# A six-layer graph network on one core: one TensorE semaphore per step in passes 1 to 4, and dense blocks streamed in 13 parts through four buffers

## Chip, core and metric

The kernel runs on one core of a Trainium2 chip, in one launch. The metric is device time in microseconds. Three timed runs of the kernel before gave 6187.99, 6189.50 and 6197.62 us, median 6189.5 us.

## What is computed

A graph of 6250 nodes with 256 features and 106250 edges (source, target, weight), sorted by target, goes through six layers with a sparse product each. Cut to what matters here:

```
A(h) = segment_sum(h[src], dst);  Aw(h) = segment_sum(w * h[src], dst);  LN = layer norm of rows
x = LN(x + rows_to_length_one(x @ Ws.T + Aw(x) @ Wn.T))                     # pass 0
h = x
for i in 0..2: h = relu(LN(relu(((1 + eps[i]) * h + A(h)) @ W1[i] + b1[i]) @ W2[i] + b2[i] + h) * gamma[i] + beta[i])   # 1 to 3
x = LN(x + h)                                                               # end of pass 3
y = (A(x * deg_out**-.5) * deg_in**-.5) @ Wgc + bgc + x @ Wres + bres       # pass 4
x = LN(x + batchnorm(y + top-2 mixture of 64 experts(y)))                   # expert stage
out = LN(x + (x - Aw(x) * (diag + 1)) @ W + bias)                           # pass 5
```

What matters for the change is A in passes 1 to 4: the same unweighted adjacency matrix times a new table of rows in each pass.

## The kernel before, in words

The targets are 49 tiles (NT) of 128 nodes. In passes 1 to 4, 29 of them are "sparse" tiles and 20 (ND) are "dense" tiles.

**Sparse tiles.** A tile has 18 columns of 128 edges, handled in six groups (GT) of three columns. For each group POOL gathers the source rows by indirect DMA (`gather`, L2228), DVE builds three one-hot "pick" matrices (`picks`, L2892, two groups ahead), and TensorE multiplies them (`products`, L2299 in passes 1 to 4, L2302 elsewhere): rows are kept as three bf16 planes, so a group is nine matmuls of 128x128 by 128x256. Slots and picks have three groups of buffers; gather and picks of group n wait on `s_prod` for the products of group n-3. A pass has 174 groups.

**Dense tiles.** For a dense tile the whole block row of the adjacency matrix, 49 blocks of 128x128 in bf16, was written to DRAM in pass 0 (`dense_blocks`, `a_dram`). In every pass from 1 to 4, TensorE multiplies all 20 x 49 = 980 blocks by the planes in SBUF (`dense`, L2323): three matmuls a block. The blocks are streamed by SP's DMA queue in QN = 10 parts per tile of four or five blocks (`load_quarter`, L2060) into three buffers AB, one in `ring` and two in `pick`. TensorE raises `s_dq` at a part's last matmul; SP waits for part n-3 before it loads part n; TensorE waits on `s_al` at a part's first block.

**The order of the work** is written out by hand as steps. `one_pass` (L2461) of TensorE in passes 1 to 4 has 183 steps: first the dense blocks of the step, six or seven of them in the first 162 (DSTEPS), then the nine products of group g, in pass 2 also six histogram matmuls (L2402), then the events of the step, then block ranks (L2331, L2335). Events belong to finished tiles: T transposes of the sums (L2417), H hidden layer (L2426), L second layer (L2441), and in pass 4 GT (L2450) and G (L2458) for the gate. They follow a tile's last product at fixed offsets (`OFFSETS`): a sparse tile ends at a step that is 5 modulo 6 and a dense tile's place is rounded up to 2 modulo 6, so that a step has at most one of T, H and L in passes 1 to 3, and at most one of them with one of GT and G in pass 4. Each kind raises a semaphore of its own: `s_prod`, `s_dq`, `s_hist`, `s_t`, `s_mm1`, `s_mm`, `s_gate`, `s_lg`.

The other engines walk through the same steps. DVE in step g builds the picks of group g+2, then does the row work of its events: Z (operand, from the finished sums), F (layer norm), R and M (splitting rows into planes), then background work (sorting edges into bins, one-hots). ScalarE copies transposes (L2627) and hidden layers (L2634) out of PSUM and takes roots (L2656). SP's queue issues in order, in each step: the parts whose buffer `quarter_done_at` places in that step, then own rows (L2052), finished rows (L2036, L2032), new planes (L2045), and rows of planes for the next pass (L2075). It reads:

```
def quarter_done_at(a):
    i, q = divmod(a, QN)
    return ((i * NT + QB[q + 1]) * DSTEPS - 1) // (ND * NT)

def blocks(g):
    return range(-(-g * ND * NT // DSTEPS), -(-(g + 1) * ND * NT // DSTEPS)) if g < DSTEPS else range(0)
```

Of the kernel before, what the change touches and what calls it, by code (L numbers as in the profile page):

```python
# [1383 lines left out]
QN = 10  # L1384
# [49 lines left out]
def gnn(nc, a, out):  # L1434
# [4 lines left out]
    with ctx:  # L1439
# [107 lines left out]
        s_al = [sem(f"dense_quarter{j}_loaded") for j in range(3)]  # L1547
        s_dq = sem("dense_quarters_done")
# [8 lines left out]
        s_prod = sem("product_groups_done")  # L1557
# [3 lines left out]
        s_mm1 = sem("first_products_done")  # L1561
# [10 lines left out]
        s_hist = sem("source_histograms_done")  # L1572
# [4 lines left out]
        s_gate = sem("gate_inputs_transposed")  # L1577
        s_gatec = sem("gate_transposes_copied")
        s_lg = sem("logits_done")
# [50 lines left out]
        AB = [v.bitcast(bf16) for v in (ring[:, SLOTS * HST // 2:SLOTS * HST // 2 + AW], pick[:, AT_AB:AT_AB + AW], pick[:, AT_AB + AW:AT_AB + 2 * AW])]  # L1630
# [229 lines left out]

        def total(k, p, w=D):

            _, q, kind, i = SEQ[k][p]
            if kind == "dense":
                n = (k - 1) * ND + i
                return bank(5 + n % 2, w), s_dq, QN * (n + 1)
# [3 lines left out]
            return bank((sparse_before(k) + i) % 2, w), s_prod, group(k, i * GT + GT - 1) + 1  # L1870
# [89 lines left out]
        def _(sp):  # L1960
# [93 lines left out]
            def load_quarter(k, a):  # L2054
                i, q = divmod(a, QN)
                n = (k - 1) * ND * QN + a
                if n >= 3:
                    sp.wait_ge(s_dq, n - 2)
                w = (QB[q + 1] - QB[q]) * P
                sp.dma_start(AB[n % 3][:, 0:w], a_dram[i][:, QB[q] * P:QB[q + 1] * P]).then_inc(s_al[n % 3], 16)  # L2060

            def load_rows(k, r):
# [7 lines left out]
                if r == 0 and k > 1:  # L2070
                    sp.wait_ge(s_dq, QN * ND * (k - 1))
# [6 lines left out]
            for k in range(5):  # L2078
# [6 lines left out]
                for q in range(3 if k in DENSE_PASSES else 0):  # L2085
# [4 lines left out]
                if k == 3:  # L2090
                    sp.wait_ge(s_hist, NH)
# [33 lines left out]
            sp.wait_ge(s_dq, QN * ND * 4)  # L2125
# [70 lines left out]
        def _(pool):  # L2196
# [71 lines left out]
        def _(pe):  # L2268
# [17 lines left out]
            def products(k, g):  # L2286
# [16 lines left out]
                last.then_inc(s_prod, 1)  # L2303

            def dense(k, g):
                for b in blocks(g):
# [6 lines left out]
                    if t == QB[q]:  # L2313
                        pe.wait_ge(s_al[quarter % 3], 16 * (quarter // 3 + 1))
# [5 lines left out]
                    block = AB[quarter % 3][:, (t - QB[q]) * P:(t - QB[q] + 1) * P]  # L2320
# [4 lines left out]
                    if t == QB[q + 1] - 1:  # L2325
                        last.then_inc(s_dq, 1)
# [72 lines left out]
            def histogram(g):  # L2399
# [4 lines left out]
                last.then_inc(s_hist, 1)  # L2404

            def transposes(k, p):
# [11 lines left out]
                last.then_inc(s_t, 1)  # L2418

            def hidden(k, q):  # L2420
# [7 lines left out]
                last.then_inc(s_mm1, 1)  # L2428

            def layer(k, q):  # L2430
# [11 lines left out]
                last.then_inc(s_mm, 1)  # L2442

            def gate_transposes(p):
# [6 lines left out]
                last.then_inc(s_gate, 1)  # L2451

            def gate(p):
# [5 lines left out]
                last.then_inc(s_lg, 1)  # L2459

            def one_pass(k):  # L2461
                for g in range(STEPS[k]):
                    if k in DENSE_PASSES:
                        dense(k, g)
                    if g < GROUPS[k]:
                        products(k, g)
# [4 lines left out]
                    if k == 2 and 5 <= g < 5 + NH:  # L2471
                        histogram(g - 5)
# [119 lines left out]
        def _(act):  # L2592
# [18 lines left out]
            def operand(p):  # L2611
# [3 lines left out]
                if n:  # L2615
                    act.wait_ge(s_t, n)
                fn(TZ[:, :], sums, ACT.Copy).then_inc(s_z, 1)

            def copy_transposes(k, q):
                n = nth(k, q)  # L2620
                act.wait_ge(s_t, n + 1)
                if k in (1, 2, 3) and q:
                    act.wait_ge(s_mm1, hid(k, q))
                elif n:
                    act.wait_ge(s_mm, n)
# [3 lines left out]
            def hidden(k, q):  # L2629
                act.wait_ge(s_mm1, hid(k, q) + 1)  # L2630
                if hid(k, q):
                    act.wait_ge(s_mm, nth(k, q))
# [817 lines left out]
```

## Time and profile before

| | |
|---|---|
| Timed runs, median of 3 | 6189.5 us (6187.99 to 6197.62) |
| Profiled execution, span | 6792.0 us |
| Mean granted TensorE clock | 0.902 |
| Setup and pass 0 | 0 to 1268 us |
| Pass 1 | 1268 to 2095 us |
| Pass 2 | 2095 to 2925 us |
| Pass 3 | 2925 to 3790 us |
| Pass 4 | 3790 to 4590 us |
| Routing, experts, batch norm, pass 5 | 4590 to 6792 us |
| TensorE matmuls in the span | 36004, busy 5260.0 us (77%) |

The profiled execution is one run under the hardware profiler; its span, from the first to the last instruction, is 602 us more than the median of the timed runs, and the profile gives no other time for it. Times of single instructions and waits come from that execution. PE is TensorE, PEld its weight loads. A wait is written as engine, its line, "<-" and what ended it: total us, times, longest. "issue" means that nothing in the profile ended the wait, "remote" a semaphore event without a releaser found.

### The profile page before, as it was taken

The numbers are of one execution on the slowest core, as the hardware profiler recorded it, in microseconds if no ns is written. First come the engines' busy times: TensorE is split into PE (matmuls) and PEld (weight loads), VectorE is DVE, ScalarE is ACT, GpSimd is POOL, SyncE is SP. The second block draws the span as 40 slices with busy tenths as digits, with TensorE's granted clock in tenths as the row PEclk, the third lists the DMA queues.
The fourth block names the chain that finished last, engine by engine and source line by source line (L and its number), as shares of the span: only waits on it lengthen the run. The fifth ranks groups of instructions, "written<-read, shape, count | busy, mean of one in ns | idle before, by whom it ended". The sixth has DMA issues, their size and how long they took to land. (4 is left out here: it accounts for less than half of the span.)

```text
span 6792.0 us, 104767 instructions
## 1 busy us (share of the span) xinstructions
PE 5260.0 (77%) x36004; PEld 4236.7 (62%) x36004; DVE 3784.2 (56%) x13501; ACT 1674.7 (25%) x4718; POOL 3742.9 (55%) x3737
## 2 busy tenths in 40 slices
PE   5888876688887888868887688880399965878787
PEld 3666664576765777647776577760388853666665
DVE  5666665476675878647776211124277745444443
ACT  3766764011110111112121000000133322222222
POOL 6666666566665666656666566651300042666665
PEclk8989997799998999989999899995699977899998
DMA  5333444666667777776666666651599952333333
GB/s 141 121 119 122 129 125 130 200 197 196 197 199 239 227 226 227 235 230 185 188 187 202 201 185 182 185 162 60 196 316 310 318 171 77 97 97 96 96 98 85
DMA packets 702175, 1180.94 MB, mean 174 GB/s; under 512 B 131306, under 2 KB 510312, under 8 KB 698924
## 3 DMA queue, kind: packets, MB, share of 16 engines
q0 software_dynamic: 212192, 625.22, 32.2%
q1 hardware_dynamic: 489450, 548.94, 25.2%
q8 instruction: 295, 4.83, 0.3%
q14 instruction: 238, 1.95, 0.1%
HBM read 1010.58 MB, written 164.46 MB: 173 GB/s over the span
## 5 line engine op out<-in xcount | busy, mean ns | idle before, releaser
L2228 POOL DMA_INDIRECT ring<-planes,REC x2088 | 2080.7, 997 | 1259.5 <-issue 542.1
L2323 PE MATMUL PS<-HH,pick 128*128 128x256 bf16 (+1 forms) x7836 | 1047.4, 278 | 193.8 <-issue 154.4
L2228 POOL DMA_INDIRECT ring<-in_x,REC x738 | 797.0, 1080 | 416.3 <-issue 195.4
L2892 DVE TENSOR_SCALAR pick<-ring,REC 128x128 bf16<-128x128 bf16 x2088 | 422.5, 265 | 1074.3 <-remote 792.7
L2323 PEld LDWEIGHTS PS<-HH,pick 128*128 128x128 bf16 x7836 | 765.5, 100 | 384.8 <-issue 221.9
L2302 PE MATMUL PS<-ring,pick 128*128 128x256 f32 x2880 | 857.5, 429 | 187.3 <-DMA ring<-table,REC 96.9
L2299 PE MATMUL PS<-ring,pick 128*128 128x256 bf16 (+1 forms) x6264 | 854.3, 279 | 104.1 <-issue 55.9
L2228 POOL DMA_INDIRECT ring<-table,REC x702 | 671.7, 957 | 454.2 <-issue 301.9
L2302 PEld LDWEIGHTS PS<-ring,pick 128*128 128x128 f32 x2880 | 573.6, 212 | 379.5 <-DMA ring<-table,REC 127.4
L2299 PEld LDWEIGHTS PS<-ring,pick 128*128 128x128 bf16 x6264 | 611.3, 99 | 249.3 <-issue 113.0
L2890 DVE TENSOR_SCALAR pick<-iota,REC 128x128 f32<-128x128 f32 x1440 | 414.7, 354 | 574.9 <-remote 272.1
L2323 PE MATMUL PS<-HH,ring 128*128 128x256 bf16 (+1 forms) x3924 | 543.8, 279 | 120.5 <-issue 84.8
L2323 PEld LDWEIGHTS PS<-HH,ring 128*128 128x128 bf16 x3924 | 383.7, 100 | 213.3 <-issue 116.7
L2251 POOL DMA_INDIRECT ring<-expert_outputs,ring x98 | 96.5, 985 | 706.0 <-DMA expert_outputs<-ring 664.7
L2385 PE MATMUL PS<-HH 128*128 128x256 f32 x1764 | 453.1, 402 | 22.1 <-ACT HH L2685 17.8
L2345 PE MATMUL PS<-HH 128*128 128x256 f32 (+3 forms) x1400 | 343.7, 362 | 125.7 <-ACT HH L2718 63.2
L2385 PEld LDWEIGHTS PS<-HH 128*128 128x128 f32 x1764 | 355.1, 204 | 80.7 <-ACT HH L2685 13.6
L2627 ACT ACTIVATE TZT<-PS 128x256 f32<-128x256 f32 (+1 forms) x294 | 132.5, 451 | 973.7 <-remote 552.9
L2345 PEld LDWEIGHTS PS<-HH 128*128 128x128 f32 (+1 forms) x1400 | 214.1, 165 | 204.5 <-issue 94.9
L2441 PE MATMUL PS<-WA,TZT 128*128 128x256 f32 x980 | 276.7, 422 | 61.5 <-ACT TZT L2627 46.7
L2529 PE MATMUL PS<-ring,HH 128*128 128x128 f32 x2240 | 277.5, 278 | 0.3 <-issue 0.3
L2441 PEld LDWEIGHTS PS<-WA,TZT 128*128 128x128 f32 x980 | 202.6, 214 | 108.6 <-ACT TZT L2627 55.6
(352 smaller groups left out, 7721.0 us busy)
## 6 DMA issues: line engine op xcount, KB each, us to landing
HH<-in_L_gnn_w SPq DMA_DIRECT2D x280, 512.0 KB, 5.1
pick<-dense_blocks SPq DMA_DIRECT2D x480, 160.0 KB
ring<-dense_blocks SPq DMA_DIRECT2D x240, 160.0 KB
HH<-planes SPq DMA_DIRECT2D x64, 576.0 KB
ring<-planes,REC POOLq DMA_INDIRECT x2088
dense_blocks<-HH SPq DMA_DIRECT2D x20, 1568.0 KB
planes<-pick SPq DMA_DIRECT2D x147, 192.0 KB
expert_inputs<-VEC SPq DMA_DIRECT2D x41, 512.0 KB
```

Source lines behind the costliest of these rows:

```text
L2228: pool.indirect_dma_start(SLOTB[:, slot, 0:RP] if dense else SLOT[:, slot, 0:D], None, planes[k] if dense else tables[k], bass.IndirectOff ...
L2251: pool.indirect_dma_start(ring[:, n % 8 * D:(n % 8 + 1) * D], None, ys_dram, bass.IndirectOffsetOnAxis(ap=GI[:, s * NT + t:s * NT + t + 1] ...
L2299: last = mm(bank(j % 2, w), PICKB[:, slot * P:(slot + 1) * P], SLOTB[:, slot, PLANE_AT[m]:PLANE_AT[m] + w], start=c == 0 and m == 0, stop= ...
L2302: last = mm(bank(j % 2, D), pick[:, slot * P:(slot + 1) * P], SLOT[:, slot, 0:D], start=c == 0, stop=c == WT - 1)
L2323: last = mm(bank(5 + n % 2, w), block, plane(m, t, w), start=t == 0 and m == 0, stop=t == NT - 1 and m == 2, skip_group_check=True)
L2345: last = mm(bank(b, w, j * 2 * P), sources[slot][:, j * P:(j + 1) * P], targets[slot][:, j * 2 * P:j * 2 * P + w], start=True, stop=not ow ...
L2385: last = mm(bank(sums_bank(v), D), AW32[f % OWN][:, s % 4 * P:(s % 4 + 1) * P], tile(X, s), start=pos == 0 and s == sources[0], stop=pos = ...
L2441: last = mm(bank(layer_bank(k), D), v, wmat(m, b), start=i == 0, stop=i == len(pairs) - 1)
L2529: last = mm(bank(3 + j, P, m * P), W1B[j][:, b * HID + m * P:b * HID + (m + 1) * P], XTB[j][:, b * P:(b + 1) * P], start=b == 0, stop=b == 1)
L2627: fn(TZT[:, 0:w], bank(2, w), ACT.Copy).then_inc(s_zt, 1)
L2890: last = v.tensor_scalar(p, iota[:, :], lo, we, ALU.is_equal, ALU.mult)
L2892: last = v.tensor_scalar(p, iotab, lo, None, ALU.is_equal)
```

## The change

In passes 1 to 4 TensorE raises only `s_prod`, once in each step that has products or an event, at the last matmul of that work. `WORK[k]` lists these steps (177, 177, 177 and 178 in passes 1 to 4). `s_dq`, `s_hist`, `s_mm1`, `s_gate` and `s_lg` are gone; `s_t` and `s_mm` stay for passes 0 and 5. Whoever waited for one of them, or for a group's products, waits for the count of its step. The dense blocks of a tile are cut into QN = 13 parts of three or four blocks, held in QA = 4 buffers; SP loads a part when the step that `quarter_done_at` gives for the part four before it is done. Block ranks still come after the increment. The diff, cut (waits of the histogram, gate, hidden layer and layer change in the same manner as those shown):

```diff
-QN = 10
+QN = 13
+QA = 4
...
+STEP_OF = [{(n, p): g for g, found in EVENTS[k].items() for n, p in found} for k in range(PASSES)]
+WORK = [sorted(set(range(GROUPS[k])) | {g for g, found in EVENTS[k].items() for n, _ in found
+                                        if k in DENSE_PASSES and n in ("T", "H", "L", "GT", "G")}) for k in range(PASSES)]
...
-        s_al = [sem(f"dense_quarter{j}_loaded") for j in range(3)]
-        s_dq = sem("dense_quarters_done")
+        s_al = [sem(f"dense_part{j}_loaded") for j in range(QA)]
...
-        s_prod = sem("product_groups_done")
+        s_prod = sem("tensor_steps_done")
...
-        AB = [v.bitcast(bf16) for v in (ring[:, SLOTS * HST // 2:SLOTS * HST // 2 + AW], pick[:, AT_AB:AT_AB + AW], pick[:, AT_AB + AW:AT_AB + 2 * AW])]
+        AB = [v.bitcast(bf16) for v in [ring[:, SLOTS * HST // 2:SLOTS * HST // 2 + AW]] +
+              [pick[:, AT_AB + j * AW:AT_AB + (j + 1) * AW] for j in range(QA - 1)]]
...
+        def step_done(k, g):
+
+            return sum(len(WORK[j]) for j in range(k)) + sum(w <= g for w in WORK[k])
+
+        def pass_done(k):
+            return step_done(k, WORK[k][-1])
+
+        def group_done(n):
+
+            k = next(k for k in range(PASSES) if n < GBASE[k + 1])
+            return step_done(k, n - GBASE[k])
+
+        def event_done(name, k, p):
+
+            return step_done(k, STEP_OF[k][name, p])
+
+        def transposed(n):
+            k, p = divmod(n - 1, NT)
+            if k in DENSE_PASSES:
+                return s_prod, event_done("T", k, p)
+            return s_t, p + 1 + (NT if k == 5 else 0)
+
+        def layer_done(n):
+            k, p = divmod(n - 1, NT)
+            if k in DENSE_PASSES:
+                return s_prod, event_done("L", k, p)
+            return s_mm, p + 1 + (NT if k == 5 else 0)
+
+        def hidden_done(n):
+            k, p = divmod(n - 1, NT)
+            return s_prod, event_done("H", k + 1, p)
+
         def total(k, p, w=D):
 
             _, q, kind, i = SEQ[k][p]
...
             if kind == "dense":
                 n = (k - 1) * ND + i
-                return bank(5 + n % 2, w), s_dq, QN * (n + 1)
+                return bank(5 + n % 2, w), s_prod, step_done(k, quarter_done_at(QN * i + QN - 1))
             if kind == "weighted":
                 v = SUMMED.index((k, q))
                 return bank(sums_bank(v), w), s_wq, NB * (v + 1)
-            return bank((sparse_before(k) + i) % 2, w), s_prod, group(k, i * GT + GT - 1) + 1
+            return bank((sparse_before(k) + i) % 2, w), s_prod, step_done(k, i * GT + GT - 1)
...
             def load_quarter(k, a):
                 i, q = divmod(a, QN)
                 n = (k - 1) * ND * QN + a
-                if n >= 3:
-                    sp.wait_ge(s_dq, n - 2)
+                if a >= QA:
+                    sp.wait_ge(s_prod, step_done(k, quarter_done_at(a - QA)))
+                elif k > 1:
+                    sp.wait_ge(s_prod, step_done(k - 1, DSTEPS - 1))
                 w = (QB[q + 1] - QB[q]) * P
-                sp.dma_start(AB[n % 3][:, 0:w], a_dram[i][:, QB[q] * P:QB[q + 1] * P]).then_inc(s_al[n % 3], 16)
+                sp.dma_start(AB[n % QA][:, 0:w], a_dram[i][:, QB[q] * P:QB[q + 1] * P]).then_inc(s_al[n % QA], 16)
...
                 if r == 0 and k > 1:
-                    sp.wait_ge(s_dq, QN * ND * (k - 1))
+                    sp.wait_ge(s_prod, step_done(k - 1, DSTEPS - 1))
...
                     if k in DENSE_PASSES:
-                        for q in range(3, ND * QN):
-                            if quarter_done_at(q - 3) == g:
+                        for q in range(QA, ND * QN):
+                            if quarter_done_at(q - QA) == g:
                                 load_quarter(k, q)
...
                 if n >= 3:
-                    pool.wait_ge(s_prod, n - 2)
+                    pool.wait_ge(s_prod, group_done(n - 3))
...
-                last.then_inc(s_prod, 1)
+                if k not in DENSE_PASSES:
+                    last.then_inc(s_prod, 1)
+                return last
...
                     if t == QB[q]:
-                        pe.wait_ge(s_al[quarter % 3], 16 * (quarter // 3 + 1))
+                        pe.wait_ge(s_al[quarter % QA], 16 * (quarter // QA + 1))
...
-                    if t == QB[q + 1] - 1:
-                        last.then_inc(s_dq, 1)
...
-                last.then_inc(s_hist, 1)
+                return last
...
-                last.then_inc(s_t, 1)
+                if k not in DENSE_PASSES:
+                    last.then_inc(s_t, 1)
+                return last
...
             def one_pass(k):
                 for g in range(STEPS[k]):
                     if k in DENSE_PASSES:
                         dense(k, g)
+                    last = None
                     if g < GROUPS[k]:
-                        products(k, g)
+                        last = products(k, g)
                     if g == 1:
                         pe.wait_ge(s_w, w_count(k))
                         if k == 0:
                             pe.wait_ge(s_wtc, 1)
                     if k == 2 and 5 <= g < 5 + NH:
-                        histogram(g - 5)
+                        last = histogram(g - 5)
                     if k == 4 and g == 3:
                         pe.wait_ge(s_bad, 1)
                         mm(bank(7, 1)[0:1, :], ones[:, 0:1], col[:, 11:12], start=True, stop=True)
@@ -2477,15 +2516,17 @@
                         mm(bank(7, NT, 128)[0:1, :], ones[:, 0:1], HELD5, start=True, stop=True).then_inc(s_badp, 1)
                     for name, p in events(k, g):
                         if name == "T":
-                            transposes(k, p)
+                            last = transposes(k, p)
                         if name == "H":
-                            hidden(k, p)
+                            last = hidden(k, p)
                         if name == "L":
-                            layer(k, p)
+                            last = layer(k, p)
                         if name == "GT":
-                            gate_transposes(p)
+                            last = gate_transposes(p)
                         if name == "G":
-                            gate(p)
+                            last = gate(p)
+                    if k in DENSE_PASSES and g in WORK[k]:
+                        last.then_inc(s_prod, 1)
...
                 if n:
-                    act.wait_ge(s_t, n)
+                    act.wait_ge(*transposed(n))
...
                 if n >= 3:
-                    dve.wait_ge(s_prod, n - 2)
+                    dve.wait_ge(s_prod, group_done(n - 3))
```

## Rows read from the trace of the kernel before

**Rows 1.** The page: its first line, busy time by engine, clock and DMA slices.
```profile
span 6792.0 us, 104767 instructions
...
PE 5260.0 (77%) x36004; PEld 4236.7 (62%) x36004; DVE 3784.2 (56%) x13501; ACT 1674.7 (25%) x4718; POOL 3742.9 (55%) x3737
...
PEclk8989997799998999989999899995699977899998
DMA  5333444666667777776666666651599952333333
```

**Rows 2.** Busy time by stretch: setup and pass 0, then passes 1 to 4.
```profile
core 0: us, PE busy (x) PEld busy (x) DVE busy (x) ACT busy (x) POOL busy (x), PEclk, DMA share, GB/s
0.00:1268.00 1268.00, 926.25 (x4280) 726.47 (x4280) 785.55 (x2646) 732.51 (x1982) 808.32 (x760) 0.88 0.43 133
1268.00:2095.00 827.00, 693.60 (x5492) 564.41 (x5492) 558.41 (x1989) 103.13 (x354) 537.08 (x515) 0.92 0.68 200
2095.00:2925.00 830.00, 692.58 (x6074) 554.96 (x6074) 584.38 (x2877) 91.71 (x296) 503.13 (x524) 0.95 0.76 230
2925.00:3790.00 865.00, 679.73 (x5472) 564.69 (x5472) 593.00 (x2128) 162.05 (x497) 542.61 (x525) 0.92 0.66 196
3790.00:4590.00 800.00, 687.73 (x5394) 563.92 (x5394) 163.04 (x676) 49.10 (x99) 489.41 (x518) 0.97 0.63 182
```

**Rows 3.** Waits of PE in 1300 to 4530 us: total, times, longest.
```profile
PE PS L2323 <- issue: 238.6, 367, 20.7
...
PE PS L2299 <- issue: 53.4, 109, 1.6
PE PS L2299 <- DMA ring<-planes,REC: 39.7, 28, 3.6
PE PS L2323 <- DMA pick<-dense_blocks: 36.2, 17, 15.9
PE PS L2441 <- ACT TM L2634: 28.5, 16, 5.2
...
PE PS L2426 <- ACT TZT L2627: 12.5, 12, 2.8
...
PE PS L2323 <- DMA ring<-dense_blocks: 8.5, 8, 3.4
```

**Rows 4.** Timeline of PE in pass 3: a whole step and its neighbours.
```profile
start us, us, engine line op out<-in xcount [idle before <-releaser]
3016.86 1.16 PE L2426 MATMUL PS<-TZT,WA 128*128 128x128 f32 x8 [0.21 <-issue]
3017.85 2.14 PE L2323 MATMUL PS<-HH,pick 128*128 128x256 bf16 x18
3019.83 1.15 PE L2299 MATMUL PS<-ring,pick 128*128 128x256 bf16 x9
3020.82 1.03 PE L2441 MATMUL PS<-WA,TM 128*128 128x256 f32 x4
...
3025.14 2.14 PE L2323 MATMUL PS<-HH,pick 128*128 128x256 bf16 x18
3027.11 1.15 PE L2299 MATMUL PS<-ring,pick 128*128 128x256 bf16 x9
3028.10 1.15 PE L2323 MATMUL PS<-HH,pick 128*128 128x256 bf16 x9
```

**Rows 5.** Timeline, pass 4: a load of a dense part and its wait.
```profile
4193.38 0.32 SPq L2060 DMA_DIRECT2D ring<-dense_blocks  x1
...
4193.96 0.38 PE L2450 MATMUL PS<-ident,HN 128*128 128x128 f32 x2
...
4195.95 0.28 PE L2323 MATMUL PS<-HH,ring 128*128 128x256 bf16 x1 [0.29 <-DMA ring<-dense_blocks]
```

**Rows 6.** Timeline, pass 1: loads behind a queue, and the wait for one.
```profile
1346.28 1.89 SPq L2060 DMA_DIRECT2D pick<-dense_blocks  x2
...
1349.54 0.82 PE L2323 MATMUL PS<-HH,pick 128*128 128x257 bf16 x3 [1.22 <-DMA pick<-dense_blocks]
```

**Rows 7.** Waits of SP's DMA queue in 1300 to 4530 us.
```profile
SPq L2060 <- remote: 1128.8, 272, 13.7
SPq L2060 <- PE PS L2323: 978.4, 342, 12.7
SPq L2036 <- DVE HN L3201: 80.2, 27, 8.7
SPq L2045 <- DVE pick L3076: 53.4, 18, 12.1
...
SPq L2032 <- DVE HN L3173: 10.0, 2, 9.5
```

**Rows 8.** Waits of DVE in 1300 to 4530 us.
```profile
DVE pick L2892 <- remote: 772.7, 273, 6.9
DVE pick L2892 <- PE PS L2299: 230.2, 104, 20.4
```

More of the change, by code:

```diff
@@ L2084, in _ @@
                     sp.dma_start(SRCI[0:EP, 0:EC], a["src"].rearrange("(p c) -> p c", c=EC)).then_inc(s_in, 16)
-                for q in range(3 if k in DENSE_PASSES else 0):
+                for q in range(QA if k in DENSE_PASSES else 0):
                     if k == 1 and q == 0:
@@ L2319, in dense @@
                         pe.wait_ge(s_rl[r % 3], 16 * (r // 3 + 1))
-                    block = AB[quarter % 3][:, (t - QB[q]) * P:(t - QB[q] + 1) * P]
+                    block = AB[quarter % QA][:, (t - QB[q]) * P:(t - QB[q] + 1) * P]
                     for m in range(3):
@@ L2427, in hidden @@
                                   start=d == 0, stop=d == 1)
-                last.then_inc(s_mm1, 1)
+                return last
             def layer(k, q):
@@ L2441, in layer @@
                     last = mm(bank(layer_bank(k), D), v, wmat(m, b), start=i == 0, stop=i == len(pairs) - 1)
-                last.then_inc(s_mm, 1)
+                if k not in DENSE_PASSES:
+                    last.then_inc(s_mm, 1)
+                return last
             def gate_transposes(p):
@@ L2450, in gate_transposes @@
                     last = nc.tensor.transpose(bank(3, P, b * P), HN[:, o + b * P:o + (b + 1) * P], ident[:, :])
-                last.then_inc(s_gate, 1)
+                return last
             def gate(p):
@@ L2458, in gate @@
                     last = mm(bank(7, NE), TM1[:, b * P:(b + 1) * P], WG[:, b * NE:(b + 1) * NE], start=b == 0, stop=b == 1)
-                last.then_inc(s_lg, 1)
+                return last
             def one_pass(k):
@@ L2620, in copy_transposes @@
                 n = nth(k, q)
-                act.wait_ge(s_t, n + 1)
+                act.wait_ge(*transposed(n + 1))
                 if k in (1, 2, 3) and q:
-                    act.wait_ge(s_mm1, hid(k, q))
+                    act.wait_ge(*hidden_done(hid(k, q)))
                 elif n:
-                    act.wait_ge(s_mm, n)
+                    act.wait_ge(*layer_done(n))
                 w = 2 * D if k in (0, 4) else D
@@ L2629, in hidden @@
             def hidden(k, q):
-                act.wait_ge(s_mm1, hid(k, q) + 1)
+                act.wait_ge(*hidden_done(hid(k, q) + 1))
                 if hid(k, q):
-                    act.wait_ge(s_mm, nth(k, q))
+                    act.wait_ge(*layer_done(nth(k, q)))
                 for b in range(2):
@@ L2640, in finish @@
                 if k == 0:
-                    act.wait_ge(s_mm, n + 1)
+                    act.wait_ge(*layer_done(n + 1))
                     if n:
@@ L2664, in gate_copy @@
             def gate_copy(p):
-                act.wait_ge(s_gate, p + 1)
+                act.wait_ge(s_prod, event_done("GT", 4, p))
                 if p:
-                    act.wait_ge(s_lg, p)
+                    act.wait_ge(s_prod, event_done("G", 4, p - 1))
                 fn(TM1[:, :], bank(3, D), ACT.Copy).then_inc(s_gatec, 1)
@@ L3146, in operand @@
                 dve.wait_ge(s, value)
-                dve.wait_ge(s_t, n)
+                dve.wait_ge(*transposed(n))
                 if k in (1, 2, 3):
@@ L3166, in finish @@
                 hn = HN[:, m % 2 * D:(m % 2 + 1) * D]
-                dve.wait_ge(s_mm, n + 1)
+                dve.wait_ge(*layer_done(n + 1))
                 if k == 4:
@@ L3213, in one_pass @@
                 if k == 1:
-                    dve.wait_ge(s_prod, group(1, 0))
+                    dve.wait_ge(s_prod, pass_done(0))
                     for j in range(2):
@@ L3336, in _ @@
             last.then_inc(s_route, 1)
-            dve.wait_ge(s_prod, group(5, 0))
+            dve.wait_ge(s_prod, pass_done(4))
             dve.wait_ge(s_b1t, 1)
```

16 lines of the change are left out of this document (6 added, 10 removed).

## Prediction

> **What bounds the kernel now.** I read the page first [rows 1]: TensorE is busy 77% of a span of 6792.0 us, more than any other engine, but unevenly. The busy time by stretch [rows 2] shows where the change acts: passes 1 to 4 take 827, 830, 865 and 800 us, 3322 in all, and TensorE has 680 to 694 us of work in each, against 537 for POOL at most and 593 for DVE. Passes 1 to 4 are bound by TensorE's own stream; a gain or a loss there is a gap taken out of that stream or put into it. The waits of TensorE [rows 3] say what the gaps are today: the largest name no releaser (238.6 us before the dense products of L2323, 53.4 before the edge products of L2299), gathers 39.7 us, hidden layers 28.5 and 12.5, and the loads of dense parts only 36.2 + 8.5 = 44.7 us in 25 gaps, 15.9 of it a single one. So three buffers of five blocks nearly hide the stream of dense blocks. The timeline of a step [rows 4] gives the pace: 18 dense matmuls (six blocks) in 1.98 us from start to start, 0.33 us a block; nine edge products in 0.99 us; then one event, 0.99 us for a hidden layer (L2426), about 1.0 for a layer (L2441), 0.38 for a pair of transposes as in [rows 5]; 0.8 on average. What stands behind the dense blocks in a step, its tail, is 0.99 + 0.8 = 1.8 us.
>
> **Semaphore increments.** TensorE raises in passes 1 to 4 696 increments after groups of products, 800 after dense parts, 637 after events (4 x 49 T, 3 x 49 H, 4 x 49 L, 49 GT, 49 G) and 147 after histograms: 2280. Of them 3 x 177 + 178 = 709 stay, so 1571 go. Their price by the rows: the run of 18 at 3025.14 covers six blocks, a part has at most five, so it has a part's increment inside, and its 18 starts take 1.97 us, as the others do; nine products that end in one take 0.99 us to the next dense matmul, 0.110 us each, the same pace [rows 4]. I take 0 us. The rows are rounded to 0.01 us, so either sign of 0.01 x 1571 = 16 us is the bound.
>
> The Trainium skill speaks here for a gain: TensorE: Matmul & The Clock Gate, section "The cost: per-tile semaphore tail", says that increments on completing matmuls serialize, at 26.3 ns each. By that figure, as an estimate, 1571 fewer would give 41 us back. The rows above do not show it.
>
> **Later signals to those who follow products.** The gathers (POOL, L2228) and picks (DVE, L2892) of group n wait for group n-3. They now wait until the event of that step is over, 0.8 us later on average. Both work with three groups of buffers, two steps ahead, a step being 827/183 = 4.5 us in the trace. DVE waits 1003 us before its picks [rows 8], and TensorE's list holds no wait for a pick at all; that cover hides it: 0 us. If it were gone, each of the 28 gaps for a gather would grow by 0.8 us, 22 us, and the 28 gaps for ScalarE's copies (16 + 12) by as much, since DVE stands in the same order before its row work: another 22. T, H, L and GT or G signals lie at the end of their step anyway, alone in it in passes 1 to 3; block ranks come after the increment. The histogram's followers already wait for that step's products. 0 us; upper bound 44, and nothing below 0, because no signal comes earlier than now.
>
> **The stream of dense parts.** This is the term that counts. A freed buffer is refilled by SP, and the question is how much TensorE work lies between the release and the first matmul of the refilled part.
> - Before: the part is released by its own last matmul, and two parts, 9 or 10 blocks, lie between. In a pass 197 loads are made so; 154 have two tails between and 43 have one: 3.2 + 3.6 = 6.8 or 3.2 + 1.8 = 5.0 us, mean 6.5.
> - After: the release is the end of the step that `quarter_done_at` names. Three parts lie between, but the rest of the step is spent before the release. That function rounds up: where a part's last block is the last of its step, it names the next step for 39 of 256 loads. Counted through the schedule, 32 loads of a pass have no tail left and 5 blocks (28) or 6 (4): 1.65 or 1.98 us, mean 1.7. The other 224 have one tail and 6 to 11 blocks: 3.8 to 5.4 us, mean 4.6.
> - What a load needs: one is issued by SP at 4193.38 and TensorE gets on at 4195.95, 2.57 us [rows 5]; another goes from 1346.28 to 1349.54, 3.26 us [rows 6]. Both are of 160 KB against some 120 KB after; I take 2.9, their mean.
> - The 32 short ones: 4 x 32 = 128 times 2.9 - 1.7 = 1.2 us is 154 us. The ends: 0, if smaller parts land in 1.7 us, and 128 x (3.26 - 1.65) = 206.
> - The 896 others: cover falls from 6.5 to 4.6 us. Today's 25 gaps arise where SP was late too; SP stands behind DVE's rows 27 + 18 + 2 = 47 times, up to 12.1 us [rows 7], while for 2107 us it stands ready at a load's wait. Leaving out the single gap of 15.9 us, 24 gaps grow by 1.9 us each: 46 us. The ends: 0, and all 47 stands, 89 us.
> - SP issues 240 loads more in the four passes, at 0.32 us each [rows 5]: 77 us in a queue that waits 2107, hidden; that cover gone they are inside the 89 above. Waiting for a step's end before the stores of that step holds these back by up to a tail; rows are read again only in the next pass, own rows only some steps later: 0, bound by the same 89.
>
> The Trainium skill weighs in on the load: DMA: Bandwidth & Descriptors, section "Anatomy of one DMA — SWDGE (gpsimd) path", puts a transfer at a fixed 2.0 us plus its bytes over 436 GB/s. As an estimate 128 KB would take 2.3 us, the short loads would cost 128 x 0.6 = 77 us, and the sum below would be 77 us less. The trace's own two loads are longer, by their rows.
>
> **Absorbed.** While TensorE waits for a part, gathers and copies catch up. The gaps that can shrink are 39.7 + 28.5 + 12.5 = 81 us; I take half, 40, with 0 and 81 as ends.
>
> **Sum:** 0 + 0 + 154 + 46 - 40 = +160 us. The profiled execution has a span of 6792.0 us and would have 6952; it is 602 us above the median of the timed runs, 6189.5, so the nameless gaps are likely to be smaller there. I carry the 160 over unchanged: 6189.5 + 160 = 6350 us, 2.6% slower. Between the ends: -16 - 81 gives -97; 16 + 44 + 206 + 89 gives +355.
>
> **Rivals.**
> - *The increments cost what the nameless gaps show (faster).* TensorE has 238.6 + 53.4 = 292 us of gaps with no releaser before its products [rows 3]. If they belonged to the increments, 1571/2280 of them, 201 us, would go, and the loads would give back only part: -201 + 160 = -41, 6148 us. It decides from the point where an increment costs over 160/1571 = 102 ns. For it: the gaps are there, and nothing else is named. Against it: the runs with an increment inside keep their pace [rows 4], and the timed runs are 602 us shorter than the profiled one, so that much of these gaps may belong to the profile. With the page's 26.3 ns it would be 160 - 41 = +119, 6308 us, still slower.
> - *The loads stay hidden (no change).* If SP's part lands within the 1.7 us, or the four buffers spare the 24 gaps of now and the rest is absorbed: 6190, within 12 us. Against it: neither load in the rows lands under 2.57 us.
> - *The step becomes a lock (much slower).* SP, POOL and DVE all hang on the step's end; if all ends of above come together, +300 to +355 us, about 6510. For it: DVE has 593 us of work in pass 3, its chain is long. Against: rows 8.
> - *The change does less than it says:* 709 of 2280 increments stay by the schedule, so that is excluded; but the loads' release may fall a step late in more cases than counted, which is the case above.
>
> **Chances.** Forecast 0.55 (6230 to 6450), lock 0.13, hidden 0.12, increments 0.20. A difference under 0.2%, 12 us, can't be told from none. Faster 0.20, same 0.12, slower 0.68. The range leaves out the greater part of the lock and half of the faster rival: 6150 to 6460.
>
> **What would show it.** Right: TensorE's waits for dense_blocks rise from 25 gaps to 100 or more, of 1 to 2 us, to some 200 us in all, spread over the four passes in a pattern of the schedule; TensorE's work per pass stays at 680 to 694 us, and its passes grow by 30 to 50 us each; pass 0, the experts and pass 5 stay. Wrong: if the nameless gaps shrink by two thirds the increments were the cost; if waits for gathers and copies grow instead of those for dense blocks, the late signals were; if loads land in under 1.7 us, nothing happens.

## The result, and the profile after

The changed kernel takes 6323.55 us (median of 4 runs, 6318.07 to 6328.31) against 6192.35 us for the kernel before on the same chip: a ratio of 1.0219, 95% interval 1.0203 to 1.0235. It is slower by 131 us. The two medians alone give 1.0212, inside the interval, so what is worked out below from 1.0219 may be 4 us too large. Forecast were 6350 us and +160 us over 6189.5.

The first profiled execution of the kernel before was unusual: no other profile here has a span so far from its timed runs as 6792.0 us. So the kernel before was profiled once more (first experiment), and this second profile, of 6189.1 us, is what the profile of after is set against. The page of after, its first lines:

```profile
span 6321.1 us, 105019 instructions
...
PE 5082.1 (80%) x36004; PEld 4181.5 (66%) x36004; DVE 3773.7 (60%) x13501; ACT 1679.3 (27%) x4718; POOL 3737.9 (59%) x3737
...
PEclk8999998899998999989999899995699997899998
DMA  5433434677778878876666776661599972333333
```

And of the kernel before in its second profile:

```profile
span 6189.1 us, 104767 instructions
...
PE 5061.4 (82%) x36004; PEld 4192.1 (68%) x36004; DVE 3774.7 (61%) x13501; ACT 1677.1 (27%) x4718; POOL 3743.3 (60%) x3737
...
PEclk8999998799998999989999899975799987899998
DMA  5443434677778888876666777751799962444433
```

The work is the same, 36004 matmuls; TensorE is busy 21 us longer, the span is 132 us longer. Busy time by stretch, after: setup and pass 0, passes 1 to 4, the rest (columns as in [rows 2]):

```profile
0.00:1213.50 1213.50, 917.81 (x4280) 713.44 (x4280) 785.79 (x2646) 733.06 (x1982) 807.51 (x760) 0.89 0.45 139
1213.50:1955.20 741.70, 644.33 (x5493) 548.17 (x5494) 555.21 (x1989) 105.97 (x354) 545.95 (x521) 0.96 0.76 226
1955.20:2726.10 770.90, 659.58 (x6075) 559.20 (x6076) 566.45 (x2877) 94.83 (x296) 496.98 (x523) 0.95 0.80 247
2726.10:3544.10 818.00, 662.39 (x5472) 560.81 (x5473) 592.55 (x2128) 162.90 (x497) 538.31 (x521) 0.93 0.69 206
3544.10:4255.00 710.90, 651.63 (x5374) 559.70 (x5375) 153.00 (x667) 42.76 (x96) 487.66 (x515) 0.98 0.69 200
4255.00:6321.00 2066.00, 1546.36 (x9314) 1240.22 (x9313) 1120.73 (x3194) 539.78 (x1493) 861.54 (x898) 0.88 0.53 166
```

The same for the kernel before, second profile, passes 1 to 4 and the rest:

```profile
1211.90:1957.80 745.90, 646.86 (x5492) 548.89 (x5493) 557.18 (x1989) 103.69 (x354) 553.91 (x522) 0.95 0.75 226
1957.80:2663.20 705.40, 645.72 (x6074) 557.93 (x6074) 565.20 (x2877) 92.31 (x296) 499.19 (x521) 0.96 0.86 269
2663.20:3466.00 802.80, 664.02 (x5472) 565.51 (x5472) 591.87 (x2128) 162.35 (x497) 533.02 (x522) 0.92 0.70 210
3466.00:4122.20 656.20, 641.29 (x5373) 560.27 (x5374) 153.96 (x667) 47.05 (x96) 487.83 (x515) 0.99 0.74 216
4122.20:6189.00 2066.80, 1542.87 (x9315) 1239.76 (x9314) 1119.89 (x3194) 538.90 (x1493) 860.84 (x898) 0.88 0.54 166
```

The loss lies in passes 2 (+65.5 us) and 4 (+54.7); pass 3 loses 15.2, pass 1 gains 4.2, and what is outside them stays within 2 us. Waits of TensorE over the whole span, after (columns as in [rows 3]):

```profile
PE PS L2359 <- DMA pick<-dense_blocks: 149.7, 114, 4.4
...
PE PS L2359 <- DMA ring<-dense_blocks: 96.2, 45, 26.5
...
PE PS L2333 <- DMA ring<-planes,REC: 71.6, 67, 3.8
...
PE PS L2359 <- issue: 55.4, 3, 19.8
PE PS L2462 <- ACT TZT L2668: 50.9, 30, 4.6
```

And before, second profile:

```profile
PE PS L2299 <- DMA ring<-planes,REC: 98.9, 118, 5.0
...
PE PS L2426 <- ACT TZT L2627: 63.2, 36, 6.0
PE PS L2323 <- issue: 55.6, 3, 19.7
PE PS L2323 <- DMA pick<-dense_blocks: 51.2, 27, 17.7
PE PS L2323 <- DMA ring<-dense_blocks: 38.9, 11, 26.7
```

TensorE waits for dense parts 159 times instead of 38, and 245.9 us instead of 90.1: +155.8 us. It waits 27.3 us less for gathers (L2333, L2299 before) and 12.3 us less for transposes copied by ScalarE. 155.8 less 27.3 and 12.3, with the 21 us of longer busy time, makes 137 us; smaller waits, 5 us less in sum, bring it to the 132 us. The 292 us before the products that nothing ended [rows 3] are down to 55.6 us in three gaps, those at the starts of passes, in both kernels.

What one late part looks like, after, in pass 4 (timeline, TensorE and SP's queue):

```profile
3708.56 1.15 PE L2333 MATMUL PS<-ring,pick 128*128 128x256 bf16 x9
3709.55 1.15 PE L2359 MATMUL PS<-HH,ring 128*128 128x256 bf16 x9
3710.53 1.15 PE L2359 MATMUL PS<-HH,pick 128*128 128x256 bf16 x9
...
3713.39 0.50 PE L2359 MATMUL PS<-HH,pick 128*128 128x256 bf16 x3 [1.71 <-DMA pick<-dense_blocks]
```

```profile
3709.74 2.21 SPq L2094 DMA_DIRECT2D pick<-dense_blocks  x2
```

A step ends with its products at 3709.7; there SP issues two loads. TensorE has six blocks left in two parts already loaded, 1.98 us from 3709.55, and stands until 3713.39. This is one of the 32 short loads of a pass, of the kind with six blocks: 3.65 us from issue to use, with 1.8 us of work for it.

The kernel's formulas tell which load each of these waits is for, since the trace has all 1040 loads and all 11760 dense matmuls in order. Of the 128 short loads TensorE waited for 115, 169.9 us in all, with a median of 3.2 us from issue to use. Of the 896 others it waited for 43, 49.5 us; one first load of a pass adds 26.5 us. Before, in the second profile, it waited for 37 of its 788 loads behind the first three of a pass, 63.4 us.

### The profile page after: what moved, and what is told of

The parts are those of the page before. It is cut to its first block, busy times and chain, and to the rows that moved or that the text cites. A ratio compares the mean times of both kernels' runs of the same rounds, so it can differ in the third digit from the quotient of the medians.

```text
span 6321.1 us, 105019 instructions
## 1 busy us (share of the span) xinstructions
PE 5082.1 (80%) x36004; PEld 4181.5 (66%) x36004; DVE 3773.7 (60%) x13501; ACT 1679.3 (27%) x4718; POOL 3737.9 (59%) x3737
## 4 chain that ended last, share of the span: by engine, by line
PE 37%; POOL 19%; DMA 14%; issue 12%; DVE 11%; ACT 5%; SPq 2%; DVEq 0%; ACTq 0%; POOLq 0%
POOL ring L2262 17%; PE PS L2359 12%; PE PS L2333 7%; DMA pick<-dense_blocks 5%; PE PS L2477 4%; DMA ring<-expert_inputs 3%; DMA ring<-dense_blocks 3%; PE PS L2336 2%; PE PS L2570 2%; PE PS L2579 2%; PE PS L2419 2%; PE PS L2462 2%; PE PS L2379 1%; POOL expert_inputs L2277 1%; DMA ring<-planes,REC 1%
## 5 line engine op out<-in xcount | busy, mean ns | idle before, releaser
L2359 PE MATMUL PS<-HH,pick 128*128 128x256 bf16 (+1 forms) x8820 | 1118.1, 276 | 150.9 <-DMA pick<-dense_blocks 149.7
L2359 PEld LDWEIGHTS PS<-HH,pick 128*128 128x128 bf16 x8820 | 853.6, 99 | 318.8 <-DMA pick<-dense_blocks 188.8
L2333 PE MATMUL PS<-ring,pick 128*128 128x256 bf16 (+1 forms) x6264 | 840.5, 278 | 73.0 <-DMA ring<-planes,REC 71.6
L2336 PEld LDWEIGHTS PS<-ring,pick 128*128 128x128 f32 x2880 | 546.6, 205 | 421.2 <-DMA ring<-table,REC 196.5
L2333 PEld LDWEIGHTS PS<-ring,pick 128*128 128x128 bf16 x6264 | 610.5, 99 | 192.6 <-DMA ring<-planes,REC 82.3
L2359 PE MATMUL PS<-HH,ring 128*128 128x256 bf16 (+1 forms) x2940 | 394.3, 276 | 151.9 <-DMA ring<-dense_blocks 96.2
L2419 PE MATMUL PS<-HH 128*128 128x256 f32 x1764 | 429.7, 386 | 0.0
L2379 PE MATMUL PS<-HH 128*128 128x256 f32 (+3 forms) x1400 | 341.6, 360 | 104.3 <-ACT HH L2759 58.6
L2359 PEld LDWEIGHTS PS<-HH,ring 128*128 128x128 bf16 x2940 | 285.0, 99 | 210.3 <-DMA ring<-dense_blocks 110.3
L2419 PEld LDWEIGHTS PS<-HH 128*128 128x128 f32 x1764 | 340.2, 195 | 47.9
L2697 ACT ACTIVATE SM<-SM 128x1 f32<-128x1 f32 x147 | 29.8, 203 | 945.4 <-DVE SM L3174 945.4
L2570 PEld LDWEIGHTS PS<-ring,HH 128*128 128x128 f32 x2240 | 269.9, 197 | 0.7 <-issue 0.7
```

Source lines behind the costliest of these rows:

```text
L2333: last = mm(bank(j % 2, w), PICKB[:, slot * P:(slot + 1) * P], SLOTB[:, slot, PLANE_AT[m]:PLANE_AT[m] + w], start=c == 0 and m == 0, stop= ...
L2336: last = mm(bank(j % 2, D), pick[:, slot * P:(slot + 1) * P], SLOT[:, slot, 0:D], start=c == 0, stop=c == WT - 1)
L2359: last = mm(bank(5 + n % 2, w), block, plane(m, t, w), start=t == 0 and m == 0, stop=t == NT - 1 and m == 2, skip_group_check=True)
L2379: last = mm(bank(b, w, j * 2 * P), sources[slot][:, j * P:(j + 1) * P], targets[slot][:, j * 2 * P:j * 2 * P + w], start=True, stop=not ow ...
L2419: last = mm(bank(sums_bank(v), D), AW32[f % OWN][:, s % 4 * P:(s % 4 + 1) * P], tile(X, s), start=pos == 0 and s == sources[0], stop=pos = ...
L2570: last = mm(bank(3 + j, P, m * P), W1B[j][:, b * HID + m * P:b * HID + (m + 1) * P], XTB[j][:, b * P:(b + 1) * P], start=b == 0, stop=b == 1)
```

## The experiments

Each run is compared with runs of the kernel before on the same chip; their medians were 6182.7, 6182.5 and 6183.8 us in the three sets.

**1. The kernel before once more.** No edit.

> The kernel before, unchanged, profiled once more: its first profile had a span 602 us above the timed runs, with 292 us of gaps before the products that nothing ended. Theory (those gaps belonged to that one execution): a span of about 6190 us, hardly any gap named issue, and the same few gaps for dense parts, 25 to 40 of them, 40 to 80 us. Rival (they belong to the kernel, to its increments): the gaps of 292 us are there again.

Measured: 6190.77 us, span 6189.1 us; the rows stand above. The nameless gaps were that one execution's. For dense parts there are 38 gaps of 90.1 us, more than the 25 of 44.7 us counted before from 1300 us on; the difference is the single gap of 26.7 us at the start of pass 1, left out there (25.8 us in the first profile), and 12 more short ones.

**2. The exact step.** In the kernel after:

```diff
+        def part_free_at(a):
+            i, q = divmod(a, QN)
+            return (i * NT + QB[q + 1] - 1) * DSTEPS // (ND * NT)
...
-                    sp.wait_ge(s_prod, step_done(k, quarter_done_at(a - QA)))
+                    sp.wait_ge(s_prod, step_done(k, part_free_at(a - QA)))
...
-                            if quarter_done_at(q - QA) == g:
+                            if part_free_at(q - QA) == g:
```

> The kernel after, with one formula changed: SP loads a part when the step in which the part's last block really runs is done, not the step that rounding up names; 39 of 256 loads of a pass are released a step earlier, and the 32 with 5 or 6 blocks of cover get a tail more. Nothing else changes, so the followers' signals and the number of increments stay. Theory of the loads: the 128 short loads cost 1.2 us each, so most of 150 us comes back less what other loads still wait: 6190 to 6250 us, and under 60 gaps for dense_blocks. Rival (late signals to gathers, picks and row work cost the time): 6310 to 6325, as after.

Measured: 6232.67 us, 1.0080 of before (1.0058 to 1.0102). Its waits for dense parts:

```profile
PE PS L2338 <- DMA ring<-planes,REC: 104.2, 123, 3.5
...
PE PS L2467 <- ACT TZT L2673: 72.3, 39, 6.1
...
PE PS L2364 <- DMA ring<-dense_blocks: 58.5, 20, 26.1
...
PE PS L2364 <- DMA pick<-dense_blocks: 37.6, 51, 3.4
```

96.1 us in 71 gaps, more gaps than the 60 expected, though shorter. By the ratios (0.0219 - 0.0080 of 6190 us) 86 us of the loss come from the 39 loads of each pass that the rounded formula releases a step late. The expectation has them wrong in one point: of the 32 short loads only the 28 with five blocks are among the 39, and they gain a whole step, six blocks and a tail. The four with six blocks are released in time by the rounded formula too and stay as short as they were; TensorE waits for 15 of these 16 here, 13.8 us. The waits for parts fall by 149.8 us from after to here and the time by less, because TensorE then stands 32.6 us longer for gathers and 21.4 us longer for transposes. The rival, that the followers' signals cost the 86 us, falls: they are unchanged here.

**3. The parts' own release.** In the kernel after:

```diff
-                if a >= QA:
-                    sp.wait_ge(s_prod, step_done(k, quarter_done_at(a - QA)))
-                elif k > 1:
-                    sp.wait_ge(s_prod, step_done(k - 1, DSTEPS - 1))
+                if n >= QA:
+                    sp.wait_ge(s_dq, n - QA + 1)
...
+                    if t == QB[q + 1] - 1:
+                        last.then_inc(s_dq, 1)
```

> The kernel after, with the semaphore of the dense parts put back: TensorE raises it at each part's last matmul (1040 increments more) and SP waits for that; 13 parts and four buffers, the one semaphore per step for all others. Theory of the loads: cover rises from a mean of 4.2 us to over 7, waits for dense_blocks all but vanish: 6170 to 6200 us. Rival (late signals of the steps cost the time): 6280 or more. Rival (an increment costs 26 ns): 27 us more than the first theory says, 6210.

Measured: 6179.85 us, 0.9993 (0.9981 to 1.0005): no different from before. Waits for dense parts:

```profile
PE PS L2358 <- DMA ring<-dense_blocks: 46.2, 6, 26.1
...
PE PS L2358 <- DMA pick<-dense_blocks: 11.9, 8, 3.9
```

The loss is in when SP may load: from this kernel to after it is 0.0226, 140 us. What one semaphore per step costs the other followers can't be read from this run alone, because the 13 parts and four buffers are in it too (experiment 5).

**4. Ten parts, three buffers.** In the kernel after:

```diff
-QN = 13
-QA = 4
+QN = 10
+QA = 3
```

> The kernel after, with the parts and buffers of before: 10 parts, three buffers, loads released by the step. Theory of the loads: two parts less the rest of the step are left as cover, under 2 us for a third of 197 loads and 3 to 4.5 for the rest, so about twice to 2.5 times the loss of the change: 6450 to 6600 us. Rival (the loss of the change comes from followers of products, or from the greater number of smaller transfers): no more than 6330.

Measured: 6535.63 us, 1.0560 (1.0536 to 1.0584), some 2.6 times the loss of the change:

```profile
PE PS L2359 <- DMA pick<-dense_blocks: 294.4, 209, 16.6
PE PS L2359 <- DMA ring<-dense_blocks: 163.1, 103, 25.3
```

With the release moved to the step's end, the 13 parts and fourth buffer are what kept the loss at 131 us.

**5. The parts alone.** The kernel before with 13 parts and four buffers:

```diff
-QN = 10
+QN = 13
+QA = 4
...
-                if n >= 3:
-                    sp.wait_ge(s_dq, n - 2)
+                if n >= QA:
+                    sp.wait_ge(s_dq, n - QA + 1)
```

> The kernel before with only the streaming changed: 13 parts, four buffers, each part still released by its own last matmul, all other semaphores as before. Theory of the loads: the finer parts and 240 more transfers cost nothing, cover stays near 7 us: 6170 to 6195 us, as the kernel with the step semaphore and the parts' own (6180). Rival (the increments have a price of 26 ns): it raises 771 increments more than that one and would be 20 us slower, 6200.

Measured: 6173.03 us, 0.9979 (0.9969 to 0.9989), a little faster than before: 58.6 us of waits for dense parts in 17 gaps instead of 90.1 in 38. Its 771 more increments than in experiment 3 cost nothing that shows. Experiment 3 is this kernel with the one semaphore per step for all followers but SP; it is 0.0014 slower, and the intervals overlap. Experiments 8 and 11 are a second such pair, 0.0022 apart the same way. Taken together, by their intervals, that is 0.0018, give or take 0.0011: the later signals cost some 11 us. The pairs were run on different chips, each against its own runs of the kernel before. The profiles put the cost in pass 3, taken from its first dense matmul to that of pass 4. It lasts 808.3 us here, and 802.8 and 807.9 in experiments 1 and 6, all with the semaphores of before. With one per step it lasts 816.0 in experiment 3, and 814.3 to 818.9 in experiments 2, 7, 9, 10 and after. TensorE stands longer for the transposes that ScalarE copies; here, then in experiment 3:

```profile
PE PS L2428 <- ACT TZT L2629: 61.2, 34, 5.6
```

```profile
PE PS L2463 <- ACT TZT L2669: 72.0, 36, 6.0
```

**6. An increment per block.** In the kernel before:

```diff
                     if t == QB[q + 1] - 1:
                         last.then_inc(s_dq, 1)
+                    else:
+                        last.then_inc(s_more, 1)
```

> The kernel before, and an increment of a semaphore that nobody waits for at every dense block that does not end a part: 3120 increments more. My step (an increment costs TensorE nothing): within 12 us of before. Rival (26.3 ns each, the figure of the Trainium skill, TensorE: Matmul & The Clock Gate, The cost: per-tile semaphore tail): 82 us more, 6265. The 102 ns from which the change would have won by its increments: 318 us more.

Measured: 6185.24 us, 1.0001 (0.9990 to 1.0013). 3120 increments more are worth +0.6 us (0.0001 of 6182.5); the upper end of the interval, 8.0 us, is 2.6 ns each. At that price the 1571 that the change takes away can bring at most 4 us; the added ones all sit on dense matmuls, those taken away also on products and events.

**7. Released at the end of the dense blocks of a step.** Over experiment 2, one semaphore more, raised once a step before the products:

```diff
-                    sp.wait_ge(s_prod, step_done(k, part_free_at(a - QA)))
+                    sp.wait_ge(s_dq, (k - 1) * DSTEPS + part_free_at(a - QA) + 1)
...
+                    if b == blocks(g)[-1]:
+                        last.then_inc(s_dq, 1)
```

> The kernel after, with one more semaphore that TensorE raises once a step, at the step's last dense matmul, before its products and event; SP waits for that of the step in which a part's last block runs. 648 increments more. Theory of the loads: the cover of the kernel with the exact step (6233) grows by one tail, 1.8 us, its least value from 3.8 to some 5.6 us: 6180 to 6195 us, under 25 gaps for dense_blocks. Rival (what is left in that kernel, 50 us, is the followers' late signals): 6225 to 6240.

Measured: 6187.99 us, 1.0006 (0.9994 to 1.0017), 15 gaps and 55.0 us for dense parts:

```profile
PE PS L2365 <- DMA ring<-dense_blocks: 46.5, 6, 27.3
...
PE PS L2365 <- DMA pick<-dense_blocks: 8.5, 9, 2.5
```

The 46 us (0.0080 - 0.0006) that separate it from experiment 2 were the tail of the step, products and event, that a release had to sit through. The least cover was not 3.8 us in experiment 2, as the expectation has it, but 2.0, for the four loads of a pass with six blocks; with a tail more it is 3.8 here.

**8. The release, and the first outputs loaded earlier.** Over experiment 3:

```diff
+XPARTS = [(0, 6)] + [(lo, min(lo + 4, NT)) for lo in range(6, NT, 4)]
+XAT = 6 + NH
...
-                if k == 3:
-                    sp.wait_ge(s_prod, step_done(2, 4 + NH))
-                    for j, (lo, hi) in enumerate(((0, GT), (GT, NT))):
...
+                    if k == 2 and XAT <= g < XAT + len(XPARTS):
+                        if g == XAT:
+                            sp.wait_ge(s_prod, step_done(2, 4 + NH))
+                        lo, hi = XPARTS[g - XAT]
+                        sp.dma_start(tiles(X[:, lo * D:hi * D], hi - lo),
+                                     tables[1][lo * P:hi * P, :].rearrange("(t p) d -> p t d", p=P)).then_inc(s_xr[lo > 0], 16)
```

> The kernel after with the parts' own release, and one thing more: the 6.3 MB of first outputs are loaded in 12 pieces in steps 153 to 164 of pass 2, after the histogram, not in two at the start of pass 3, where a part waits behind them for 17.7 us. If that gap is on the path: 15 to 18 us less than with the release alone, 6160 to 6165. Rival (pass 3 is held by the row work and takes the gap back, as it took back most of the change's waits): 6175 to 6185.

Measured: 6171.56 us, 0.9985 (0.9975 to 0.9995). By the ratios it is 5 us under experiment 3 (0.0008 of 6182.5); the intervals overlap, so this run alone leaves it open, and it lies between what the theory and the rival expected. The single wait of 17.7 us for a part in pass 3 of experiment 3 is gone from its profile, so most of that wait did not come back as time.

**9 and 10. The step's release in two passes only.** Over experiment 3, with (1, 3) and then (2, 4):

```diff
-                if n >= QA:
+                if k in (1, 3) and a >= QA:
+                    sp.wait_ge(s_prod, step_done(k, quarter_done_at(a - QA)))
+                elif n >= QA:
                     sp.wait_ge(s_dq, n - QA + 1)
```

> The kernel after; parts are released by the step's end in passes 1 and 3, by their own last matmul in 2 and 4. Theory (passes 1 and 3 are held by ScalarE's and DVE's row work and background, which take the loads' waits back): 10 us over the kernel with the parts' own release everywhere (6180), so 6185 to 6200. Rival (each pass pays for its own waits alike, and their lengths in the profiles differ by chance): half of the 141 us, 6240 to 6260.

> The same, turned round: step's end in passes 2 and 4, own release in 1 and 3. Theory: nearly all of the change's loss, 130 us: 6300 to 6315. Rival: half of it, 6240 to 6260.

Measured: 6198.23 us, 1.0023 (1.0011 to 1.0035), and 6312.88 us, 1.0208 (1.0184 to 1.0232). Against experiment 3 (0.9993) that is 19 us for passes 1 and 3 and 133 us for passes 2 and 4. The sizes came as expected; the holder that I had named is right for one pass only. Waits of TensorE in pass 1, from its first products on, before (second profile), then after:

```profile
PE PS L2299 <- DMA ring<-planes,REC: 50.9, 56, 5.0
PE PS L2323 <- DMA pick<-dense_blocks: 20.3, 13, 3.3
PE PS L2323 <- DMA ring<-dense_blocks: 3.9, 1, 3.9
```

```profile
PE PS L2359 <- DMA pick<-dense_blocks: 36.0, 26, 3.4
PE PS L2333 <- DMA ring<-planes,REC: 23.6, 23, 2.5
PE PS L2359 <- DMA ring<-dense_blocks: 13.8, 10, 2.2
```

In pass 1 it is the gathers: waits for parts grow by 25.6 us, those for gathers shrink by 27.3. In pass 3 it is the row work, as I had thought: parts +34.6 us, while these waits, the first row of that pass before and after, shrink by 12.0 and the pass grows by 15.2. Most of those 15.2 us are not the parts': with the parts' own release (experiment 3) pass 3 already takes 816.0 us of the 818.0 after.

```profile
PE PS L2426 <- ACT TZT L2627: 62.0, 33, 6.0
```

```profile
PE PS L2462 <- ACT TZT L2668: 50.0, 28, 4.6
```

In passes 2 and 4 TensorE waits for little else before, 18.0 and 13.3 us for gathers, and the parts' +50.6 and +45.5 us go straight to the end.

**11. The parts alone, and the first outputs loaded earlier.** Experiment 5 with the same move as experiment 8.

> The kernel before with 13 parts and four buffers and its own semaphores, and the first outputs loaded in 12 pieces late in pass 2. Theory (the two add up): 13 us less than before for the parts, 8 for the load: 6160 to 6170. Rival (they save the same gap, pass 3 gives nothing more): as the parts alone, 6173.

Measured: 6161.75 us, 0.9963 (0.9950 to 0.9976), the fastest of all, 22 us under the kernel before of its set. Together the two edits beat both kernels; what the early load adds to the parts alone, 0.0016, is not settled, as the two intervals overlap. The long wait in pass 3, 16.1 us in experiment 5, is gone here too.

## Why the prediction was right

The mechanism and the time came as forecast: SP's loads wait for a step's end, and TensorE stands for the short ones. That the sum came so close is in part luck, since one term was 60 us too high and others were too low.

**Increments: 0 us, right.** Taken from the pace of matmuls in [rows 4], with 16 us as bound; experiment 6 puts 1571 of them at 4 us at most. The rival that gave them the nameless gaps falls by experiments 1 and 6: the gaps were not there a second time, and more increments bring none. So does the figure of the Trainium skill, TensorE: Matmul & The Clock Gate, section "The cost: per-tile semaphore tail": 26.3 ns each would have been 82 us for 3120, measured +0.6. The section is about many small tiles that complete together; here each increment has full 128x256 matmuls behind it.

**Later signals to gathers, picks and row work: 0 us, nearly right** (bound 44). Two pairs of experiments (3 and 5, 8 and 11) put them at some 11 us, in pass 3, where TensorE waits for the row work. Waits for gathers are nearly the same in experiments 3 and 5, 123.5 and 120.6 us, so the cover of two steps held for those. Which of the signals to the row work makes the 11 us was not separated.

**The short loads: 154 us, right.** 128 of them were to wait 1.2 us each. TensorE waited for 115 of them, 169.9 us. Pass 4 of after, where little else is in the way, shows it best, 37 gaps of 46.2 us for parts:

```profile
PE PS L2359 <- DMA pick<-dense_blocks: 34.8, 25, 2.0
...
PE PS L2359 <- DMA ring<-dense_blocks: 11.4, 12, 1.7
```

30 of these gaps, 41.6 us, are for the pass's 32 short loads. Over all passes the 112 with five blocks make 154.0 us and the 16 with six 15.9. Only the 112 come from `quarter_done_at` rounding up to the next step. Undoing it alone (experiment 2) brought 86 us of time back; 54 us went into longer waits for gathers and transposes.

**The other loads: 46 us, wrong.** The prediction let the gaps of today grow with the cover that these loads lose, 1.9 us for each of 24 (the means behind it are 6.4 and 4.5 us by its own counts, not 6.5 and 4.6; the difference stands). They did not grow: the 896 others show 49.5 us of waits after, where all 788 loads of before show 63.4, so this part fell by 14 us. The two terms together were to bring 200 us of new waits for parts; there are 155.8.

**The time of a load: 2.9 us, a little low.** The short loads that TensorE waited for took 3.2 us, by their median. By the figure of the Trainium skill, DMA: Bandwidth & Descriptors, section "Anatomy of one DMA — SWDGE (gpsimd) path", a fixed 2.0 us plus bytes over 436 GB/s, the sum would have been +83 us. That section is about transfers issued by GpSimd and these are SP's; the traces' own loads gave the better estimate here.

**Absorbed: 40 us, right** by size: 27.3 + 12.3 = 39.6. But half of the available gaps spread over all passes was not how it went: pass 1 took back all of its own, pass 3 most, passes 2 and 4 nothing. So the passes did not grow by 30 to 50 us each, as the signs of being right had it, but by -4, 65, 15 and 55.

**What the sum left out: a longer busy time.** TensorE is busy 21 us longer for the same matmuls, 13.9 of it in pass 2 and 10.3 in pass 4 (in passes 1 and 3 it is a little less busy). Part of it is how the profile counts: nine products last 1.15 us where the next work starts after 0.99 [rows 4], so each gap adds some 0.16 us of busy time. With 33 gaps more in pass 2 and 29 in pass 4 that is, as an estimate, 10 us of the 24. Another part is the clock: in pass 2 TensorE is busy for 45.3 us at the lower level, 1.2 GHz, instead of 29.0, in pass 4 for 9.0 instead of 3.6, and the granted clock goes from 0.96 to 0.95 and from 0.99 to 0.98. Nine products that last 1.15 us at the higher level last 2.13 at the lower one (after, at 2345.92 us, granted clock 0.50), so about half of the additional time, 11 us, is what that costs, as an estimate. The clock falls ten times within pass 2 of after, seven times right behind a wait of 2.0 to 4.4 us for a dense part; before it falls five times, once behind such a wait. That these waits lowered it is likely by this, but no run separates it.

The terms in order, forecast and measured: short loads 154 and 170, other loads 46 and -14, absorbed -40 and -40, nothing and -5 for smaller waits, nothing and +21 for busy time; 160 forecast, 132 in the spans. In time, by the ratios, the change is -13 us for the 13 parts and four buffers (experiment 5), +9 for the later signals (from 5 to 3) and +140 for SP's release (from 3 to after); that is 136 by the ratio of 1.0219, 131 by the medians. The reading of the profile's extra 602 us, that the nameless gaps would be smaller in the timed runs, fits the second profile, where they are 55.6 us.

## What to carry to other kernels

When releases of a streamed buffer are merged into a coarser signal, count for every load the work between the new signal and the first use, and compare it with the time from issue to landing; the mean cover (4.2 us here) hides the few loads that have 1.7, and a rounding in the schedule can make those. A semaphore increment on a matmul showed no cost here, so merging increments bought nothing, while later signals cost some 11 us and the later release of a buffer 140; here the release was best given at the buffer's last reader. And a wait cost its time in full only in the passes where the waiting engine had no other wait to give back.

## What the runs showed of the hardware that was not expected

One profiled execution of the kernel before was 602 us longer than its timed runs, with 292 us in gaps before TensorE's products that nothing in the profile ended, while a second one matched the timed runs to 2 us. The mean of a dense matmul was 278 and 276 ns, but TensorE's busy time was 199 us apart and its idle time more; what made the first execution longer is not known. So the span is to be compared with the timed runs before any share is taken from a profile.

3120 more semaphore increments on matmuls changed the time by 0.6 us, at most 2.6 ns each (experiment 6).
